# Cross-attention block: row sums by VectorE's transpose and joins, and a re-ordered first batch

## The reference

```
memory_proj    = memory @ W_mem^T                                # 1601 x 512
scores         = x @ memory_proj^T / sqrt(512)                   # 512 x 1601
attn           = softmax(scores)                                 # over the 1601
memory_context = attn @ memory_proj                              # 512 x 512
gate           = sigmoid([x, memory_context] @ W_gate^T + b_gate)
fused          = x + gate * memory_context
out            = fused * rsqrt(mean(fused^2) + 1e-6) * norm_w
```

## Time and profile before

| | |
|---|---|
| median of 3 runs | 537.66 us (537.37 to 537.76) |
| the profiled execution | 537.72 us, span 535.9 us |
| granted TensorE clock, mean | 0.996 |
| TensorE busy | 524.8 us, 98% |
| VectorE busy | 482.8 us, 90% |
| ScalarE busy | 323.2 us, 60% |
| GpSimd busy | 172.2 us, 32% |

### The profile page before, as it was taken

How to read it: one execution, slowest core, us unless ns; L and a number is a source line. 1 busy time by engine, 2 the same in 40 slices (tenths; PEclk the granted TensorE clock), 3 DMA queues, 4 the chain that set the end, 5 groups by cost and what they waited for, 6 DMA issues and landing times.

```text
span 535.9 us, 8824 instructions
## 1 busy us (share of the span) xinstructions
PE 524.8 (98%) x2364; PEld 431.7 (81%) x2364; DVE 482.8 (90%) x797; ACT 323.2 (60%) x614; POOL 172.2 (32%) x129
## 2 busy tenths in 40 slices
PE   8998999999999999999999999999999999999994
PEld 7876888888888888888888888888888888888883
DVE  3799958999799998999989998899979999899967
ACT  4675636676467655686465863666557765558524
POOL 0004610185004740066200950027400573008702
PEclk9999999999999999999999999999999999999998
DMA  9967263511687027840378105870267502401033
GB/s 226 269 122 125 64 102 91 100 40 31 181 164 130 20 59 168 177 81 20 112 149 185 39 20 173 148 144 21 75 153 167 110 20 76 141 31 39 2 117 119
DMA packets 186118, 56.38 MB, mean 105 GB/s; under 512 B 161756, under 2 KB 175592, under 8 KB 186100
## 3 DMA queue, kind: packets, MB, share of 16 engines
q1 hardware_dynamic: 185572, 55.64, 44.7%
q10 hardware_dynamic: 528, 0.52, 0.3%
HBM read 46.15 MB, written 8.39 MB: 102 GB/s over the span
## 4 chain that ended last, share of the span: by engine, by line
PE 93%; DVE 4%; DMA 1%; issue 1%; ACT 1%; SPq 0%; POOLq 0%; POOL 0%; DVEq 0%
PE bank L391 22%; PE bank L393 21%; PE bank L392 21%; PE bank L567 8%; PE bank L568 8%; PE bank L569 8%; PE bank L470 1%; DMA mem_raw<-in_ctx_dram 1%; PE bank L551 1%; PE bank L550 1%; PE bank L603 0%; DVE wg1t_lo L904 0%; DVE p_lo L904 0%; DVE fused L1081 0%; SPq L339 0%
## 5 line engine op out<-in xcount | busy, mean ns | idle before, releaser
L1256 POOL TENSOR_TENSOR psum_rows<-psum_rows,p_tmp 128x512 f32<-128x512 f32 (+1 forms) x88 | 129.6, 1473 | 39.5 <-ACT p_tmp L735 36.1
L904 DVE TENSOR_TENSOR p_lo<-p_tmp,p_hi 128x512 fp32r<-128x512 f32 (+1 forms) x104 | 89.2, 858 | 5.9 <-ACT p_hi L696 5.9
L1267 POOL TENSOR_TENSOR fused<-fused,x_again 128x512 f32<-128x512 f32 x14 | 17.9, 1300 | 219.1 <-DVE fused L1077 219.1
L391 PE MATMUL bank<-q_hi,mt_hi 128*128 128x512 f32 (+1 forms) x208 | 81.9, 394 | 0.0
L393 PE MATMUL bank<-q_hi,mt_lo 128*128 128x512 f32 (+1 forms) x208 | 81.3, 391 | 0.0
L392 PE MATMUL bank<-q_lo,mt_hi 128*128 128x512 f32 (+1 forms) x208 | 81.2, 390 | 0.0
L735 ACT ACTIVATE p_tmp<-s 128x512 f32<-128x512 f32 (+1 forms) x104 | 64.4, 626 | 27.6 <-DVE s L968 26.5
L567 PE MATMUL bank<-p_hi,mem_hi 128*128 128x512 f32 (+1 forms) x196 | 76.4, 390 | 0.0
L568 PE MATMUL bank<-p_lo,mem_hi 128*128 128x512 f32 (+1 forms) x196 | 76.3, 390 | 0.0
L569 PE MATMUL bank<-p_hi,mem_lo 128*128 128x512 f32 (+1 forms) x196 | 76.3, 389 | 0.0
L696 ACT ACTIVATE s<-bank 128x512 f32<-128x512 f32 (+1 forms) x104 | 62.0, 596 | 19.1 <-PE bank L393 18.7
(11 more groups left out here) (105 smaller groups left out, 1024.7 us busy)
## 6 DMA issues: line engine op xcount, KB each, us to landing
mem_raw<-in_ctx_dram SPq DMA_DIRECT2D x48, 256.0 KB, 3.0
mem_blocks<-in_ctx_dram SPq DMA_DIRECT2D x64, 136.0 KB
x_again<-in_x_dram SPq DMA_DIRECT2D x32, 256.0 KB, 2.8
out_dram<-fused SPq DMA_DIRECT2D x32, 256.0 KB, 2.1
x_raw<-in_x_dram SPq DMA_DIRECT2D x112, 64.0 KB, 2.0
mem_blocks<-in_ctx_dram SPq DMA_DIRECT2D x56, 64.0 KB, 2.0
x_raw<-in_x_dram SPq DMA_DIRECT2D x4, 256.0 KB, 4.9
gate<-in_L_xattn_W_gate_dram SPq DMA_DIRECT2D x2, 512.0 KB, 5.9
```

What stands on the lines that cost most here:

```text
L391: nc.tensor.matmul(dst, a_hi, b_hi, start=(start and i == 0), stop=False)
L904: return nc.vector.tensor_tensor(dst, src, hi.bitcast(F32), ALU.subtract)
L1256: nc.gpsimd.tensor_tensor(psum_rows[0:r, :], a, p_tmp[0:r, t % TMP_RING, :], ALU.add).then_inc(p_added, 1)
```

## The change

- **Row sums, all batches but the last.** The four matmuls go. At the end of a batch's VectorE order, ahead of `u_lo_part`, `transpose_sums` transposes psum_rows in 32x32 blocks into bank 7. In the next batch's score stage `reduce_sums` (pair step 1) sums each block's rows, `join_sums` (pair step 3) adds the halves of the partitions and then, by four operations on 32 partitions each, puts the sums of the four x tiles where they belong, and `reciprocal` (pair step 5) reads them from SBUF. Until now it came after `column_max`. The last batch keeps the matmuls. TensorE's `context` of tile 1 waits for `reduce_sums` (it writes bank 7), and GpSimd's first add of a batch waits for the transpose in place of the matmuls.
- **First batch, gate banks.** gate_x uses banks 2, 4, 5, 2; only tile 3 waits for an `add_bias`, that of tile 0.
- **First batch, splits.** VectorE's splits of memory pairs 4, 5 and 6 are done at softmax steps 4, 6 and 7 (`FIRST_SPLITS`); before, 4 and 5 ended the score stage and 6 stood at step 5. ScalarE's halves stay where they were.
- **First batch, weights.** The four weight clusters between score tiles come after tiles 7, 8, 10 and 11 in place of 7, 8, 9 and 10.
- **First batch, ragged tile.** It is stacked as in the others: SP does `stack_last_tile(0)` ahead of the loop, and ScalarE takes q_hi and mt_hi after the last p_hi; before, q_hi stood ahead of the last p_hi. VectorE takes mt_lo ahead of q_lo.

```diff
-        GX_BANKS = (0, 1, 2, 4)
+        GX_BANKS, FIRST_GX_BANKS = (0, 1, 2, 4), (2, 4, 5, 2)
...
-        WG2T_AT = [7, 8, 9, 10]
+        WG2T_AT = [7, 8, 10, 11]
...
+        FIRST_SPLITS = {4: [4], 6: [5], 7: [6]}
...
+            stack_last_tile(0)
             with sp.Fori(1, B - 1) as b:
...
                 else:
-                    row_sums(b - 1, True)
                     gate_context(b - 1, 0)
...
+                if j == 1 and not tail:
+
+                    pe.wait_ge(sum_reduced, b + 1)
...
-                    elif j >= 2:
-
-                        pe.wait_ge(gx_done, NT * b + j - 1)
+                    elif j == 3:
+
+                        pe.wait_ge(gx_done, NT * b + 1)
...
-                    if first or t < MT - 1:
+                    if t < MT - 1:
                         weighted(b, t)
...
-                        if not last and t == 12:
-                            q_hi_part(b + 1, 0)
-                            q_hi_part(b + 1, 1)
...
+            def transpose_sums(b):
+
+                dve.wait_ge(p_added, (MT - 1) * (b + 1))
+                dve.wait_ge(xt_has_lo, DT * (b + 2))
+                nc.vector.transpose(blocks(bank[SUM_BANK][:, :]), blocks(psum_rows[:, :])).then_inc(sum_blocks, 1)
+
+            def reduce_sums(b):
+
+                dve.wait_ge(sum_blocks, b + 1)
+                nc.vector.tensor_reduce(sum_parts[:, :], blocks(bank[SUM_BANK][:, :]), AX.X, ALU.add).then_inc(sum_reduced, 1)
+
+            def join_sums(b):
+
+                dve.wait_ge(sum_reduced, b + 1)
+                nc.vector.tensor_tensor(sum_pairs[:, :], sum_parts[0 : P // 2, :], sum_parts[P // 2 : P, :],
+                                        ALU.add).then_inc(sum_paired, 1)
+
+                dve.wait_ge(sum_paired, b + 1)
+                pairs = sum_pairs[:, :].rearrange("p (j a) -> p a j", a=BLOCKS)
+                for a in range(BLOCKS):
+                    nc.vector.tensor_tensor(p_total[a * BLOCK : (a + 1) * BLOCK, :], pairs[0:BLOCK, a, :],
+                                            pairs[BLOCK : 2 * BLOCK, a, :], ALU.add).then_inc(summed, 1)
...
+                    if not first and p == 1:
+                        reduce_sums(b - 1)
+                    if not first and p == 3:
+                        join_sums(b - 1)
+                    if not first and p == 5:
+                        reciprocal(b - 1)
...
-                    for q in (SPLIT_BY_SCORES if p < MP - 1 or first else {}).get(p, []):
+                    for q in (SPLIT_BY_SCORES if p < MP - 1 else {}).get(p, []):
                         mem_lo_part(b, q)
...
-                        for q in SPLIT_BY_SOFTMAX.get(t, []):
+                        for q in FIRST_SPLITS.get(t, []):
                             mem_lo_part(b, q)
...
                     column_max(b)
-                    reciprocal(b - 1)
                     gate_input(b - 1, 0)
...
                 if not last:
-                    q_lo_part(b + 1, 0)
-                    q_lo_part(b + 1, 1)
                     if first:
                         mt_lo_part(b + 1, 0)
                         mt_lo_part(b + 1, 1)
+                    q_lo_part(b + 1, 0)
+                    q_lo_part(b + 1, 1)
+                if not last:
+                    transpose_sums(b)
...
-                        pool.wait_ge(pe_sum, b)
+                        pool.wait_ge(sum_blocks, b)
```

More of the change, by code:

```diff
@@ L122, in xattn_kernel @@
         r_sum = sb("r_sum", [P, NT])
+        sum_parts = sb("sum_parts", [P, N // BLOCK])
+        sum_pairs = sb("sum_pairs", [P // 2, N // BLOCK])
+        p_total = sb("p_total", [P, NT])
         r_half = sb("r_half", [P, NT])
@@ L134, in xattn_kernel @@
         QX_BANKS = (2, 4)
-        GX_BANKS = (0, 1, 2, 4)
+        GX_BANKS, FIRST_GX_BANKS = (0, 1, 2, 4), (2, 4, 5, 2)
         TAIL_G_BANKS, TAIL_CTX_BANKS = (4, 5, 2, 3), (6, 7, 0, 1)
         def gx_bank(j, first):
-            return bank[QX_BANKS[j % 2] if first else GX_BANKS[j]]
+            return bank[(FIRST_GX_BANKS if first else GX_BANKS)[j]]
         def g_bank(j, tail):
@@ L202, in xattn_kernel @@
         scaled = sem("scaled")
+        sum_blocks, sum_reduced, sum_paired, summed = (
+            sem("sum_blocks"), sem("sum_reduced"), sem("sum_paired"), sem("summed"))
         normed, tail_done = sem("normed"), sem("tail_done")
@@ L545, in weighted_last_tile @@
                 t, k = MT - 1, LAST + REST
-                pe.wait_ge(stacked, 64 * b)
+                pe.wait_ge(stacked, 64 * (b + 1))
                 for c in range(CT):
@@ L859, in iteration @@
                             xt_hi_part(b + 1, X_AT.index(t - 1), False)
[L860 to L865, removed]
+                if not last:
                     mt_hi_part(b + 1, 0)
                     mt_hi_part(b + 1, 1)
+                    q_hi_part(b + 1, 0)
+                    q_hi_part(b + 1, 1)
                 for c in range(CT):
@@ L904, in lo_part, with blocks @@
                 return nc.vector.tensor_tensor(dst, src, hi.bitcast(F32), ALU.subtract)
+            def blocks(ap):
+                return ap.rearrange("p (r i) -> p r i", i=BLOCK)
             def running_max(b, t):
@@ L929, in mem_lo_part @@
                 lo_part(mem_lo[0:r, ts, :], mem_raw[0:r, raw, :], mem_hi[0:r, ts, :]).then_inc(mem_has_lo, 1)
-            def blocks(ap):
-                return ap.rearrange("p (r i) -> p r i", i=BLOCK)
             def column_max(b):
@@ L1010, in u_lo_part, with reciprocal @@
                 lo_part(u_lo[:, c, :], bank[U_BANK + c][:, :], u_hi[:, c, :]).then_inc(u_has_lo, 1)
-            def reciprocal(b):
-                dve.wait_ge(pe_sum, b + 1)
-                nc.vector.reciprocal(r_sum[:, :], bank[MAX_BANK][:, 0:NT]).then_inc(r_first, 1)
+            def transpose_sums(b):
[14 more added lines that the diff above has]
+                                            pairs[BLOCK : 2 * BLOCK, a, :], ALU.add).then_inc(summed, 1)
+            def reciprocal(b, tail=False):
+                if tail:
+                    dve.wait_ge(pe_sum, 1)
+                    total = bank[MAX_BANK][:, 0:NT]
+                else:
+                    dve.wait_ge(summed, BLOCKS * (b + 1))
+                    total = p_total[:, :]
+                nc.vector.reciprocal(r_sum[:, :], total).then_inc(r_first, 1)
                 dve.wait_ge(r_first, b + 1)
@@ L1214, in _ @@
             iteration(B - 1, False, True)
-            reciprocal(B - 1)
+            reciprocal(B - 1, True)
             gate_input(B - 1, 0, True)
```

10 lines of the change are left out of this document (4 added, 6 removed).

## The result

The changed kernel takes 535.01 us, the median of 5 runs (534.80 to 535.09), against 537.67 for the kernel before on the same chip (537.37 to 538.48, 5 runs). The ratio is 0.9948, 95% interval 0.9934 to 0.9962: 2.7 us or 0.5% faster. The forecast was 532.3, in a range of 530.3 to 535.8: the direction and the range held, the forecast gain was twice the real one.

A forecast was written before the change was run, and what follows sets the result against it. TensorE, busy for 98% of the span, was taken to bound the kernel, until VectorE, with 4.1 us to spare, would. 537.72 less 4.9 (row sums) less 0.5 (first batch) gave 532.3 us; eight in ten, 530.3 to 535.8.

The forecast's parts named there:

- Row sums: Matmuls leaving TensorE save 0.91 us per batch; less a stall, 4.3 us over six batches plus 0.6 in the last: 4.9.
- The stall: Steady batches: TensorE waits ahead of the scores for a late q_lo; bounds 0.05 and 0.95 us per batch, taken as 0.2.
- the relief that the prediction expected from the port: Steady batches: earlier xt_hi and exps shift the VectorE-GpSimd port waits, which can give back about 0.6 us.
- R3: Rival: VectorE paces all batches, blocked splits making the stall 0.95 us per batch; 536.8 us, chance 0.12.
- Last batch: The last batch gains 0.6 us from the row sums, its u_lo standing behind outputs that VectorE makes anyway.
- First batch: Banks, moved splits, clusters and stacked tile save 1.2 us, less 0.65 for one blocked split: 0.5 us saved.
- the prediction's 1.2: First batch: query starts 0.74 us earlier, plus 0.46 from the ragged tile, if the moved splits cost 0.6 each.
- One blocked split costs 0.65. I take one: First batch: one of the moved VectorE splits is held by a GpSimd add, costing 0.65 us.
- R2: Rival: GpSimd's adds block each of the first batch's three splits by 0.8 us; 534.0 us, chance 0.18.
- The first stall: First batch: TensorE's 0.5 us loss ahead of gate_x goes, as column_max starts 1.1 us earlier without two memory splits.
- R1: Rival: TensorE keeps setting the pace, joins cheap, stall 0.05 us, first batch saves 1.2; 530.6 us, chance 0.25.
- R4: Rival: VectorE's additions make q_lo 1.6 us late, 0.7 lost net in each of 6 batches; 541.4 us, chance 0.04.

The follow-up runs named there:

- Experiment 9: experiment 6 with, in all batches but the first, VectorE's split of memory pair 3 moved from the score stage to softmax step 6; 534.66 us.
- experiment 5: experiment 1 with the last batch's first u_lo put behind the second of the four outputs instead of the fourth; 530.91 us.
- experiment 2: The kernel before with only the row sums moved to VectorE, the rest of the change taken out; 532.71 us.
- experiment 1: The changed kernel with the first batch's splits of memory pairs 4, 5 and 6 back where they stood before the change; 531.61 us.
- experiment 3: The changed kernel with GpSimd adding only 8 of 512 columns in the first batch from tile 2 on (its row sums wrong); 531.19 us.
- experiment 7: experiment 1 with one more 128x512 reduce per batch on VectorE, into a buffer nobody reads; 535.84 us.
- Experiment 11: experiment 6 with the four small joins all on partitions 0 to 31 (row totals wrong); 529.61 us.
- experiment 6: experiment 5 with the first batch's pair 4 split in the score stage and pairs 5 and 6 at softmax step 11; 530.11 us.
- experiment 8: experiment 1 with the four weight clusters of the first score stage back after tiles 7, 8, 9 and 10; 531.50 us.
- experiment 10: experiment 1 with the ragged tile of the first batch not stacked (6 matmuls for 4, no stacking copies); 532.15 us.

## Why the prediction was half right

**Row sums, 4.9 us forecast, 5.0 measured; the sum right in part by luck.** TensorE is rid of 0.90 per batch, where 0.91 was worked out. The stall was taken as 0.2; 0.91 less 0.82 leaves 0.1. That is 0.6 us more than forecast over six batches, and the last batch gave 0.5 less: the two misses cancel. Transpose and reduce cost 0.62 and 0.59 (0.63 and 0.62 forecast), the joins 0.96 (1.0). The forecast had VectorE 0.5 us late at the gate input. It is 22.38 us behind the first score (229.43 less 207.05, kernel after), where it was 22.06 before: 0.3 late. The place was wrong. The wait of the steady batches, 0.16 to 0.19 us of the loads, stands ahead of the third gate matmul group (`gate_context` of x tile 2), released by the gate input, whose semaphore is z. That is one of the prediction's own signs of a wrong mechanism, and it came about, if small. In the last batch it is longest, timeline of TensorE's loads, kernel after:

```profile
479.82 0.19 PEld L400 LDWEIGHTS bank<-v_hi,u_hi 128*128 128x128 f32 x1 [0.36 <-DVE gate L1052]
```

q_lo has no wait, because of the relief that the prediction expected from the port, at its size of 0.6. Timelines of VectorE, kernel before and then after, sixth softmax step of the fourth batch, with GpSimd's add of the kernel after last:

```profile
247.13 0.66 DVE L904 TENSOR_TENSOR mem_lo<-mem_raw,mem_hi 128x512 fp32r<-128x512 f32 x1
...
248.91 1.29 DVE L904 TENSOR_TENSOR p_lo<-p_tmp,p_hi 128x512 fp32r<-128x512 f32 x1
```

```profile
248.08 0.66 DVE L905 TENSOR_TENSOR mem_lo<-mem_raw,mem_hi 128x512 fp32r<-128x512 f32 x1
...
249.86 0.66 DVE L905 TENSOR_TENSOR p_lo<-p_tmp,p_hi 128x512 fp32r<-128x512 f32 x1
```

```profile
248.18 1.72 POOL L1292 TENSOR_TENSOR psum_rows<-psum_rows,p_tmp 128x512 f32<-128x512 f32 x1 [1.29 <-ACT p_tmp L742]
```

Before, p_lo took 1.29 us. After it takes 0.66 at the same step, and the split starts 0.1 ahead of GpSimd's add at 248.18, which is the longer one now (1.72). The way there is the predicted one too: ScalarE's xt_hi, released by TensorE, starts 40.67 us behind the batch's first score before (247.09) and 39.86 after (246.91), and the exp behind it, and so the add, is earlier with it. In the third batch q_lo starts 61.03 us behind the first score (205.73 less 144.70), where it was 61.35 (204.61 less 143.26). Experiment 9 shows what was hanging on this: with its splits held, a batch is 0.8 us longer (63.14 for 62.33), R3's mechanism and near R3's size.

**Last batch, 0.6 of the 4.9 forecast, 0.1 measured; wrong.** The sentence that its u_lo "stands behind the outputs that VectorE makes anyway" was read as harmless. With the row sums gone from behind the last scores, TensorE comes to the tail 0.9 us sooner. The four outputs wait for GpSimd's r_rms and come 55.54 us behind the batch's first score (511.98 less 456.44), where it was 54.91, so u_lo behind them is late. That costs 0.6 us, which experiment 5 brings back, and the wait ahead of the gate input shown above costs another 0.3: nothing is left of the 0.9.

**First batch, -0.5 forecast, +2.3 measured; the step that failed.** Taken without the moved splits, banks, clusters and stacked tile give 64.47 - 63.27 = 1.20 us (experiments 2 and 1): the banks 0.85, the stacked tile 0.46, the clusters -0.1. That this is the prediction's 1.2 is in part luck, for the prediction had the moved splits in it, at 0.6 each against 1.1 from an earlier column_max. The loss was mis-sized. The term said "One blocked split costs 0.65. I take one". No row has the 0.65; the prediction's own rows give 0.79 (1.45 less 0.66). And all three are blocked: the move costs 3.4 us by experiment 1. The rows say how. Timelines of VectorE, the p_lo of tile 9, which releases TensorE's last wait ahead of the query, kernel after and then experiment 1:

```profile
71.08 0.66 DVE L905 TENSOR_TENSOR p_lo<-p_tmp,p_hi 128x512 fp32r<-128x512 f32 x1
```

```profile
67.58 0.66 DVE L905 TENSOR_TENSOR p_lo<-p_tmp,p_hi 128x512 fp32r<-128x512 f32 x1
```

It is 3.5 us later. The three splits are held for 0.79, 0.79 and 1.08 us, 2.7 together. The first two also bring their own 1.2 us into this stage, where column_max is only 0.5 earlier (38.12 for 38.60), and held p_lo add 0.1: 2.7 + 1.2 - 0.5 + 0.1 = 3.5. Against the forecast, the held splits are 2.0 us of the miss and column_max 0.7.

The sentence above the term already said where GpSimd's add falls, "just where a moved split stands". The paragraph behind it worked out from the Trainium skill, SBUF — State Buffer, section "Who interferes with whom", that all three would be blocked. By that rule, the trace and experiment 3 agree: 1.46, 1.45 and 1.50 us with the adds, 0.67, 0.66 and 0.42 without. That GpSimd is busy for only a third of a batch, the argument against R2, was worth nothing: both engines do one round per tile, each add and the split behind it follow the same shift of the scores, and so the distance between them is the same each time (0.39, 0.40, 0.39 us). Three of three met. Even R2 was short. It had 2.4 us for the three splits; the small third one is held for 1.1 us, not 0.8, and the move brings less at its other end. The first stall did go but for 0.2 us of the loads, but column_max comes only 0.4 us earlier than in the kernel before (38.12 for 38.51), not 1.1, since it waits 0.56 for the last running max.

**The rivals.** R1 (TensorE sets the pace, 530.6) is as near as the forecast for the steady batches, whose 62.34 us lies between its 62.25 and the forecast's 62.4, and wrong for the first. R2 (534.0) is right in its mechanism and nearest in its time; it had a chance of 0.18, and the measured 535.0 is inside the stated range because the range was drawn to take R2 in. R3 and R4 did not come about, but experiment 7 shows how near they are: VectorE's slack for work ahead of the gate input is nil, although it is idle for 2.35 us of each batch.

**The joins.** Forecast at their upper value, 0.2 each, and right: 0.19. By the rule of the Trainium skill, VectorE: DVE Perf Modes, section "Two Vector instructions with no wait between them", an instruction whose operands start in another group of 32 partitions is held until the earlier ones have finished. Experiment 11 agrees: 0.19 each with changing groups, 0.08 with one. It changed the groups that are read and those that are written together, so it doesn't show which of them matters.

**Open.** The division of the 3.4 us is read from the rows of two executions; no run took the parts from each other. By it the move would cost 0.7 us (1.2 less 0.5) even if no split were held, and no run shows that either, as experiment 3 freed tile 2's p_lo as well.

## What to carry to other kernels

When instructions on VectorE and GpSimd follow the same event round after round, work out the distance of the pair once and price either all of them as colliding or none, not a share by how busy GpSimd is; the cure is to place VectorE's two-input SBUF work where the other engine rests (experiment 6), and not to make it shorter: the smallest split was held as long as the others. Slack is counted to the next demand of the busiest engine, stage by stage: VectorE's 2.35 us of idle per batch bore not one more reduce. A stage that is emptied on one engine meets the next engine's pace, so a removed stall of 1.7 us was worth 0.85.

## What was not expected of the hardware

A held instruction pays for what is left of the other, whatever its own length: the split of 65x256 took 1.50 us for 0.40, longer than the two of 128x512, as the add that held it took 1.60 in place of 1.29. Why that add was longer is not known.

One execution of experiment 8 lost 1.5 us in its tail. Stretches view of that execution, then TensorE's first matmuls of the second stretch:

```profile
509.00:511.70 2.70, 2.39 (x15) 1.80 (x13) 2.65 (x5) 0.87 (x2) 0.00 (x0) 1.00 0.66 247
511.70:515.10 3.40, 3.40 (x8) 2.70 (x9) 0.95 (x3) 0.32 (x1) 0.00 (x0) 0.53 0.78 267
```

```profile
511.70 0.66 PE L400 MATMUL bank<-v_hi,u_hi 128*128 128x512 f32 x1 [0.31 <-DVE u_lo L905]
512.16 0.63 PE L401 MATMUL bank<-v_lo,u_hi 128*128 128x512 f32 x1
```

Behind a wait for u_lo that leaves TensorE busy for 2.39 of 2.70 us, the granted clock is 0.53, the level of 1.2 GHz, for 3.4 us, and matmuls start 0.43 apart instead of 0.23. In experiment 5, which has no such wait, the clock is full over the same stretches. Experiment 1 has the wait too (TensorE busy for 2.45 of the same 2.70 us), as has the kernel after, and both kept the clock at 1.00 in their profiled executions, so the wait does not bring it about each time. Whether it is needed is open too: experiments 5 and 10 each have one execution, not profiled, that is 1.5 to 1.8 us longer than their others, and 5 has no wait. What decides was not tried.
